# Splitting two waits of a transformer block's TensorE queue in half, and moving one GpSimd bias add behind a split

## What is computed

```python
# x (2, 1024, 256), context (2, 77, 192), 8 heads of 64; FFN 256 -> 1024 -> 256
x = x + softmax(q k^T / 8) v @ Wo + bo          # q from layernorm(x), k and v from context
h = layernorm(x) * ln_gamma + ln_beta
w1, w2 = dequant(fc1_q, fc1_scales), dequant(fc2_q, fc2_scales)   # (q - 128) * scale
y = silu(h @ w1 + fc1_bias)
x = x + 0.5 * (y @ w2 + fc2_bias)
```

## Time and profile before

| | |
|---|---|
| median of 3 runs | 192.18 us |
| profiled execution, device time | 192.23 us |
| its span in the profile | 190.4 us |
| PE busy | 183.5 us (96%) |
| DVE, ACT, POOL busy | 123.5, 122.9, 116.5 us |
| chain that ended last, share of PE | 85% |
| chain that ended last, share of DVE | 10% |

### The profile page before, as it was taken

How to read it: one execution, slowest core, us unless ns; L and a number is a source line. 1 busy time by engine, 2 the same in 40 slices (tenths; PEclk the granted TensorE clock), 3 DMA queues, 4 the chain that set the end, 5 groups by cost and what they waited for, 6 DMA issues and landing times.

```text
span 190.4 us, 3884 instructions
## 1 busy us (share of the span) xinstructions
PE 183.5 (96%) x1502; PEld 179.8 (94%) x1502; DVE 123.5 (65%) x261; ACT 122.9 (65%) x230; POOL 116.5 (61%) x159
## 2 busy tenths in 40 slices
PE   7999899899899999999999999999999999999994
PEld 6999699699899999999999999999999999999894
DVE  0287987999879364946496459745793767165341
ACT  3287970799738970898188836894389727952580
POOL 5032998389975966297809871697359653768020
PEclk9999999999999999999999999999999999999999
DMA  6996990000000100010001000100010000100101
GB/s 160 318 397 183 333 363 17 2 0 3 2 0 23 35 0 0 3 55 0 3 0 55 3 0 0 60 2 0 0 35 23 0 3 0 55 3 0 55 3 55
DMA packets 9480, 10.72 MB, mean 56 GB/s; under 512 B 2268, under 2 KB 8183, under 8 KB 9335
## 3 DMA queue, kind: packets, MB, share of 16 engines
q1 hardware_dynamic: 8837, 9.70, 15.5%
q10 hardware_dynamic: 626, 0.79, 1.4%
HBM read 8.38 MB, written 2.10 MB: 55 GB/s over the span
## 4 chain that ended last, share of the span: by engine, by line
PE 85%; DVE 10%; DMA 2%; issue 1%; ACT 0%
PE T L826 22%; PE H L814 21%; PE S L781 13%; PE T L802 13%; PE S L788 4%; PE S L734 3%; DMA ctx_sb<-in_ctx 2%; DVE w_lo L610 2%; PE H L753 2%; DVE hT_lo L592 1%; PE H L765 1%; PE T L765 1%; DVE q_sb L604 1%; PE T L719 1%; PE H L719 1%
## 5 line engine op out<-in xcount | busy, mean ns | idle before, releaser
L293 POOL TENSOR_TENSOR y_lo<-y,y_hi 128x512 fp32r<-128x512 f32 x28 | 37.6, 1364 | 3.2 <-ACT y_hi L413 3.0
L814 PE MATMUL H<-hT_hi,w_hi 128*128 128x256 f32 x128 | 37.2, 291 | 1.2 <-issue 0.8
L261 POOL TENSOR_TENSOR probs<-probs,rsum 128x616 f32<-128x616 f32 x16 | 19.2, 1220 | 31.3 <-DVE rsum L562 31.3
L826 PE MATMUL T<-w_hi,y_hi 128*128 128x256 f32 x128 | 36.8, 287 | 0.5 <-DVE w_lo L610 0.5
L814 PE MATMUL H<-hT_hi,w_lo 128*128 128x256 f32 x128 | 35.7, 279 | 0.0
L826 PE MATMUL T<-w_lo,y_hi 128*128 128x256 f32 x128 | 35.6, 279 | 0.0
L826 PE MATMUL T<-w_hi,y_lo 128*128 128x256 f32 x128 | 35.6, 278 | 0.0
L814 PE MATMUL H<-hT_lo,w_hi 128*128 128x256 f32 x128 | 35.6, 278 | 0.0
L409 ACT ACTIVATE y<-H,vec 128x256 f32<-128x256 f32 x64 | 26.6, 469 | 8.3 <-PE H L814 8.3
L382 ACT ACTIVATE probs<-probs,rstd 128x616 f32<-128x616 f32 x16 | 12.9, 807 | 27.4 <-DVE probs L550 27.4
L814 PEld LDWEIGHTS H<-hT_hi,w_hi 128*128 128x128 f32 x128 | 24.1, 188 | 1.8 <-issue 1.2
(11 more groups left out here) (127 smaller groups left out, 461.0 us busy)
## 6 DMA issues: line engine op xcount, KB each, us to landing
q_sb<-in_L_ffn_fc_q SPq DMA_DIRECT2D x2, 1024.0 KB, 8.3
out_x<-x_sb SPq DMA_DIRECT2D x16, 128.0 KB, 1.8
x_sb<-in_x SPq DMA_DIRECT2D x7, 256.0 KB, 8.3
s_sb<-in_L_ffn_fc_scales SPq DMA_DIRECT2D x2, 512.0 KB, 12.4
s_sb<-in_L_ffn_fc_scales SPq DMA_DIRECT2D x1, 1024.0 KB, 7.9
wq_sb<-in_L_xattn_Wq SPq DMA_DIRECT2D x1, 512.0 KB, 6.1
wo_sb<-in_L_xattn_Wo SPq DMA_DIRECT2D x1, 512.0 KB, 8.6
wk_sb<-in_L_xattn_Wk ACTq DMA_DIRECT2D x1, 384.0 KB, 4.6
```

What stands on the lines that cost most here:

```text
L261: nc.gpsimd.tensor_tensor(p, p, rsum[:, j, :].unsqueeze(2).to_broadcast([P, HEADS, J]), ALU.mult).then_inc(norm_done, 1)
L293: nc.gpsimd.tensor_tensor(y_lo[:, two, :], y[:, two, :], f32(y_hi[:, two, :]), ALU.subtract).then_inc(y_lo_done, 1)
L814: ins = mm(r[:, q * W:(q + 1) * W], wt[:, c, m * P:(m + 1) * P], ht[:, c, :], start=i == 0, stop=i == len(steps) - 1)
L826: ins = mm(o, yt[:, m, j * P:(j + 1) * P], wt[:, m, :], start=m == 0 and i == 0, stop=m == M - 1 and i == 2)
```

## The change

There are three edits.

1. The first layer waits only for the first chunk of h before it begins. A new semaphore, h_half_split, tells of it, and the wait for the bank, so for the second chunk, stands behind the first six matmuls. For that the loops in `fc1` are turned: chunk c outside, output half q inside. Since both output halves of a bank are now open together, only the very first matmul of the twelve carries the start flag, and only the last one the stop flag.
2. The second layer of pair 0 waits for the first half of w2 ahead of chunk 0 and for the second half ahead of chunk 4, where it waited for both ahead of chunk 0.
3. In the last turn of its loop, POOL waits until the last pair's h is split before it adds the bias to the pair before.

```diff
                     rsqrt2(a)
+                    if a == LAST:
+                        wait_freed(pool, f"HT{LAST}")
                     add_b2(a - 1)
...
                         ins = nc.vector.tensor_tensor(hT_lo[:, c, :], hT[:, c, :], f32(hT_hi[:, c, :]), ALU.subtract)
-                    ins.then_inc(freed[place[f"HT{a}"][0]], 1)
+                        ins.then_inc(h_half_split if c == 0 else freed[place[f"HT{a}"][0]], 1)
...
                     if p == 0:
-                        wait_freed(pe, f"HT{f}")
+                        pe.wait_ge(h_half_split, f + 1)
                     r = emptied(name)
-                    steps = [(wt, ht, c) for c in range(C) for wt, ht in ((w1_hi, hT_hi), (w1_hi, hT_lo), (w1_lo, hT_hi))]
-                    for q in range(2):
-                        m = 2 * p + q
-                        for i, (wt, ht, c) in enumerate(steps):
-                            ins = mm(r[:, q * W:(q + 1) * W], wt[:, c, m * P:(m + 1) * P], ht[:, c, :], start=i == 0, stop=i == len(steps) - 1)
+                    for c in range(C):
+                        if p == 0 and c == 1:
+                            wait_freed(pe, f"HT{f}")
+                        for q in range(2):
+                            m = 2 * p + q
+                            for i, (wt, ht) in enumerate(((w1_hi, hT_hi), (w1_hi, hT_lo), (w1_lo, hT_hi))):
+                                ins = mm(r[:, q * W:(q + 1) * W], wt[:, c, m * P:(m + 1) * P], ht[:, c, :], start=c == q == i == 0, stop=c == q == 1 and i == 2)
                     fill(name, ins)
...
                     for m in ms:
+                        if f == 0 and j == 0 and m % (M // 2) == 0:
+                            pe.wait_ge(w2_split, m // (M // 2) + 1)
...
-                pe.wait_ge(w2_split, 2)
                 fc2(0, 0)
```

More of the change, by code:

```diff
@@ L185, in build_program @@
         res_rstd_done = sem("res_rstd_done")
-        h_done, h_hi_done, res_part, res_done = sem("h_done"), sem("h_hi_done"), sem("res_part"), sem("res_done")
+        h_done, h_hi_done, h_half_split, res_part, res_done = sem("h_done"), sem("h_hi_done"), sem("h_half_split"), sem("res_part"), sem("res_done")
         y_hi_done, y_lo_done = sem("y_hi_done"), sem("y_lo_done")
```

## The result

The changed kernel takes 191.27 us (median of 14 runs; 192.34 for the kernel before, beside it on the same chips). The ratio is 0.9932, with a 95% interval of 0.9905 to 0.9958. So the gain between the medians is about 1.0 us. The two ratios say more than that (0.9932 of 192.3 us is 1.3 us), because they lie near the ratios of the means, 0.9935 and 0.9919, and some executions take about 1.9 us more: 2 of 14 before and 1 of 14 after in the first measurement, 4 of 13 and none of 10 in the second, by their times with the late start that is told at the end. Without them the medians differ by 1.0 and 0.9 us.

What follows compares the result with a forecast made beforehand. PE, busy 96% of the span, was taken to bound the kernel. Terms 0.00 + 0.00 + 0.07 + 0.30 = 0.37 us off 192.23 gave 191.86, or 191.8 us for the median; range 191.3 to 192.2.

Steps and rivals of the forecast that it cites:

- Parts 1 and 2: First pair, half waits for h and w2: 0.00 us each, as POOL's normalization and bank T0 are late next.
- Part 3: Pairs 1 to 5, half of h: small stops of 0.05 us go, 0.25 us freed, 0.07 us left after the pace.
- Parts 3 and 4, the pace: Behind removed stops matmuls keep the slower pace: 0.18 us given back in two pairs, 0.38 us in the last.
- the middle: From the start of pair 0's second layer to the transposes of pair 7's h: forecast gain 0.07 us.
- Part 4: Last pair: the idle stop before its first layer vanishes, freeing 0.68 us, 0.30 us after the slower pace.
- The tail: From the transposes of pair 7's h to the start of the last matmul: forecast gain 0.30 us.
- B: Rival, chance 0.34: pace behind the vanished stops is faster or soon becomes so; gain 0.75 to 0.93 us, 191.35.
- A: The forecast itself, chance 0.51: stops go and the slow pace carries on; 191.8 us, range 191.55 to 192.0.
- either edit alone: Last pair: half of h, or POOL's add behind the split, each by itself covers the 0.68 us.
- Part 5: First layer, turned loops: 64 more changes of output half cost 0, bounds 0 and 0.26 us in all.
- The added waits on PE: Counted as 8 on PE; claimed to be met before they are read, save where told.

Runs made afterwards that it cites:

- e10: The kernel before with the second edit alone (w2 in halves); 192.38 us in one execution.
- e4: The changed kernel with DVE's attention add of pair 1, tile 0, moved ahead of the second w2 subtraction; 191.40 us against 192.54, ratio 0.9920.
- e2: The kernel before with the half wait for h alone, in the old loop order; 191.46 us against 192.54, ratio 0.9940.
- e8: The kernel before, full wait, with three more matmuls between h's transposes and the first layer at pairs 1 to 5; 192.10 us, ratio 0.9974.
- e9: The full change again, unchanged, beside the kernel before (the second measurement); 191.51 us against 192.44, ratio 0.9916.
- e3: The kernel before with the third edit alone (POOL's bias add behind the split of h); 192.32 us against 192.54, ratio 0.9973.
- e5: The changed kernel without edits 2 and 3 (half of h with turned loops); 191.68 us against 192.49, ratio 0.9963.
- e1: The kernel before with the first layer's loops turned and the full wait kept; 192.45 us against 192.54, ratio 0.9989.
- e6: The kernel before with half of h in the old loop order and POOL's add behind the split; 191.63 us against 192.49, ratio 0.9946.
- e7: The kernel before once more, unchanged, one execution for its trace; no total time given, middle 123.69 us, tail 14.79 us.

## Why the prediction was right or wrong

**Parts 1 and 2, 0.00 us each: right, and shown.** The second five transposes wait for POOL in the changed kernel, and the second layer waits for bank T0 (e10, e4).

**Part 3, the stop: right. Parts 3 and 4, the pace: wrong.** The stops of 0.05 us at pairs 1 to 5 are gone with half of h (e2) and also with cover (e8). The failing step is the one that begins "Pair 6 is the only one whose first layer follows the second layer of another pair without a stop, and it is slow", and goes on to "If they carry it to the end". From one stretch I made a rule, that the first layer keeps the pace of the second layer ahead of it, and ran it over the whole kernel: two fast stretches would turn slow, and 96 matmuls with them. The twelve traces hold 84 such passages (pairs 1 to 7). In all of them the last twelve steps of the second layer are slow, 0.118 us, and yet the stretches that follow without a stop are fast 44 times and slow 8 times. Behind a small stop (second step of 0.135 to 0.177 us) they are fast 13 times and slow 14 times (one of the 13 is e2's last pair, which has a larger stop behind it), behind the stop of 0.6 us fast 4 times and slow once. So a small stop costs its 0.05 us and, about every other time instead of one time in six, another 0.1 us of pace over 24 matmuls; taking it away brings both. I had the sign of the second term the wrong way round.

The counts by place are less even. At pairs 1 to 5, 31 of 35 stretches are fast without a stop and 12 of 25 with one, which is the comparison that carries the sentence above. At pair 6, which never has a stop, 10 of 12 are fast. At pair 7 without a stop it is only 3 of 5, and the changed kernel itself shows both (fast in its first trace, slow in e9), so for the 96 last matmuls the traces don't say which outcome is the usual one.

In numbers: the middle was to gain 0.07 us. It gained 123.72 - 123.17 = 0.55 between the two first traces, and 0.45 between the means of the five kernels with the small stops (123.68) and the five with half of h and an unchanged front (123.23). That term was mis-sized by a factor of six. The five stops are 0.25 us of it. Slow stretches at pairs 1 to 6 went from 15 of 30 to 2 of 30, so 2.6 fewer for each kernel at 24 x 0.0044 = 0.1 us, which is about 0.27 us more: an estimate of 0.5 for the 0.45 measured.

**Part 4, the large stop: right.** DVE's 1.56 us was POOL's add, and 0.68 us is what its removal frees. The tail gained 14.77 - 14.11 = 0.66 us in the first trace, which is B, and 14.77 - 14.51 = 0.26 in the second, which is A's 0.30. Here A was one of two real outcomes, not the rule. That either edit alone would do was right for the stop, but not with the same margin. POOL's move alone leaves 0.6 us: in e3 the second half is split at 174.94 + 0.42 = 175.36 us and the first layer starts at 175.98. Half of h alone leaves none, as e5's stop of 0.02 us shows, and with three matmuls in place of six it leaves a stop (e2).

**Part 5, the order of the loops: right,** 0 (e1, e6). The added waits on PE are nine and not eight, since the second layer of pair 0 has one more; that changes nothing in the sum.

**The sum.** 0.45 for the middle and 0.26 to 0.66 for the tail is 0.7 to 1.1 us, and the medians show 1.07 and 0.93. The chances put 0.34 on B, whose gain of 0.75 to 0.93 us off 192.18 is 191.25 to 191.43, and that holds the result. The mechanism was on the list, and the weight went to the wrong side because of one row. But that B's span holds the time is in part luck: the kernel before took 192.34 beside the change, and the gain of 1.07 us is over B's 0.93, since B too gave the middle no more than the 0.25 us of its stops. The range left B's lower edge out on purpose, and that is where the time fell.

**What stays open.** What makes a stretch fast or slow isn't known. The only sign found is in the steps themselves: of the stretches without a stop, the eight slow ones all follow a step of 0.115 us into the first layer and go on with 0.116 or 0.117, and the 44 fast ones begin with a step of 0.121 to 0.124. That describes the two courses and doesn't explain them. Nor do the traces tell whether a stop reaches beyond its own pair: pair 6 is fast in 3 of the 5 kernels with small stops at pairs 1 to 5, and in all 7 without them, which is too few to tell.

## What to carry to other kernels

When an engine is 96% busy, look at its steps and not only at its waits: five stops of 0.05 us that no view of waits lists cost this kernel about twice their length (0.45 us), because of the pace behind them. Before a sum rests on how a stretch behaves in a new place, count how many such stretches the trace holds; a single one is an anecdote, and its two outcomes belong in the range. And where a wait is shortened, ask per place what is late next: at pair 0 POOL's normalization and a bank freed by DVE stood right behind the two waits that were shortened, and nothing was gained there.

## What the runs showed of the hardware that I had not expected

The same 256-column matmul with its weight load runs at a step of 0.1133 or 0.1177 us at one granted clock (1.00 in both), holds its pace over up to 96 matmuls, and may change it where it is started anew or passes from one layer to the next: from slow to fast at 44 of the 52 passages without a stop from the second layer of one pair to the first layer of another, but never at the 12 from the first to the second layer of pair 7. It differs between executions of one kernel, and over the 96 last matmuls it is worth 0.4 us. The Trainium skill, "TensorE: Matmul & The Clock Gate", section "Back-to-back issue gap", has one spacing for a number of columns; the two measured steps don't fit that, and the measurement decides.

The start of the kernel differs between executions too: in the traces of e1 and e7 the first projections ran at twice the step, and all behind them came 1.8 to 2.0 us later. In the timeline of e7 eight matmuls take 2.39 us (second line below) where the first trace of before has 1.29 (first line); the granted clock from 5 to 8 us is 1.00 in both, so it doesn't tell why.

```profile
5.76 1.29 PE L719 MATMUL T<-ctxT,wk_sb 96*128 96x154 f32 x8 [0.21 <-ACT ctxT L425]
...
6.16 2.39 PE L719 MATMUL T<-ctxT,wk_sb 96*128 96x154 f32 x8
```

Of all the executions measured, 3 of 64 took over 193 us with a kernel that waits for half of h, and 30 of 115 with one that doesn't. That difference is what parts the ratios of the first section from the medians. The late start lies before anything that the change touches, and no run here tells whether the change has a part in it.
